# Two slots of a routed feed-forward layer started ahead of the last routing, V weights loaded in place, and the attention's values projected by channel

## Chip, core and metric

The kernel runs on one core of a Trainium2 chip. The metric is the device time of one launch, in microseconds (us). All tensors are float32; every large product is made of three matmuls of "fp32r" operands, a high part times high part, and the two products of a high with a low part.

## What is computed

Input x is 2 x 2048 x 256. The program is a feed-forward layer with three experts, a causal attention with one head of 128, and the same feed-forward layer again (same weights).

```python
x = x + 0.5 * ffn(layernorm(x)); x = x + attention(layernorm(x)); x = x + 0.5 * ffn(layernorm(x))
# ffn(x):
att = sigmoid(ln(x) @ Wr) * (ln(x) @ Wv) @ Wo;  state = ln(x) @ Ws;  x = x + att;  h = ln2(x)
bids = conf * shares * sigmoid(h @ w_diff) + h @ W_aff          # conf = sigmoid(h @ conf weights)
winner = argmax(bids)
hr[e] = square(relu(h @ K[e]));  out[e] = hr[e] @ V[e]          # experts 0, 1: 256 -> 1024 -> 256
out_trans = (h @ W1 * sigmoid(state @ W2)) @ W3                 # expert 2
return x + out[winner] * scale
```

## The kernel before, in words

Each feed-forward layer (FFN) has two stages. Stage A (ffn_a_*) goes over the 4096 rows in NG = 8 groups of 512, in a software pipeline written out by hand for each engine. For a group it makes the gates (U, Wo), the second normalization, its transpose hT, the bids, the W1 and W3 products of expert 2, and the rank of each row within expert 0 or 1 (prefix, rank). GpSimd scatters the finished rows (257 columns of h and index, 257 of residual and gate) with indirect DMAs to a DRAM array routed_rows, where the rows of expert 0 grow from one end and those of expert 1 from the other. Groups 0 to 5 are scattered whole (scatter, four DMAs of 128 rows), groups 6 and 7 in halves (scatter_half 0 and 1): half 0, what the expert products need, first; half 1 only when win_second and w3 on DVE have put the gate and expert 2's share into the rows (semaphore rdone).

Stage B (ffn_b_*) goes over NSLOT = 17 slots of 256 routed rows (the last of 128). DVE makes a table (flag, start) that says each slot's expert and first tile, from the number of rows of expert 1, known after the last group. SyncE loads the rows of a slot (slot_z: the h half; slot_row: the other half). For slot j, PE transposes (sT), ScalarE and DVE split the transpose into shT_hi and shT_lo (shi, slo), PE multiplies with K (Kj: four quarters of 12 matmuls of 256 columns in banks 1 to 4), ScalarE takes relu and hr_hi, DVE the square (sq), GpSimd hr_lo (hrlo), then PE multiplies with V (Vj: 48 matmuls), DVE adds the residual (orow) and GpSimd sends the rows with indirect DMAs (send). PE's order in a body is Kj(j), sT(j+1), Vj(j-1). sq of quarters 2 and 3 of slot j waits for hrlo of quarters 0 and 1 of the same slot (two buffers); on DVE slo(j+1) stands behind sq(j), and PE's Kj(j+1) waits for slo(j+1). On GpSimd a body is hrlo(j), a drain, send(j-1).

All orders are the order of the code. Before the change stage B begins when the table is done and the halves 0 of all groups have landed. In the first FFN the K, V and attention weights are loaded late in stage A (late_sync) into space that stage A has given back, and split into high and low parts by ScalarE (split_hi) and DVE (split_lo); the K bias is made by 64 matmuls of one column (k_bias). In the second FFN the weights are there.

The attention projects Q, K and V for 16 blocks of 256 rows (project_qk, project_v), eight ahead of the scores, the others one by one between them. project_v makes rows of values: 12 matmuls with a 128 x 128 tile of the normalized rows standing and 128 weight columns moving.

## Time and profile before

| what | us |
|---|---|
| three timed runs: median (lowest to highest) | 1061.05 (1060.47 to 1067.13) |
| the profiled execution, its own time | 1064.8 |
| its span (first to last instruction) | 1063.0 |
| first FFN (stage A to about 189, stage B to about 413) | 413 |
| attention | 413 to about 665 |
| second FFN (stage A to about 840) | 665 to 1063 |

The mean granted TensorE clock is 0.972 of full speed. In the rows below, times are us from the start of the span unless marked ns; PE is TensorE's matmul stream, PEld its weight loads, DVE is VectorE, ACT ScalarE, POOL GpSimd, SP SyncE. A row of the timeline gives start, duration, engine, line, operation, output<-inputs and count, and in brackets the idle time ahead of it and what ended it. Matmuls overlap in a pipeline, so the distance of two starts, not the duration, is what a matmul costs.

### The profile page before, as it was taken

What the parts mean: (1) busy time and instruction counts of PE and PEld (TensorE: products, weight loads), DVE (VectorE), ACT (ScalarE), POOL (GpSimd) and SP (SyncE); (2) the same over time, 40 slices, a digit from 0 to 9 for tenths busy, and PEclk for the clock granted to TensorE, in tenths of its full rate; (3) what the DMA queues carried; (4) which work ended last, traced back from release to release, by engine and by line L of the source; (5) the groups of instructions that cost most, each with busy time, mean ns of one, the idle gap of its engine ahead of it and who ended that gap; (6) DMA issues with size and microseconds to landing.
All of it is one profiled execution on the core that took longest, in us unless ns stands there. A gap on an engine that the chain in (4) does not pass through costs nothing.

```text
span 1063.0 us, 21617 instructions
## 1 busy us (share of the span) xinstructions
PE 988.0 (93%) x7024; PEld 912.5 (86%) x7025; DVE 688.6 (65%) x1762; ACT 560.1 (53%) x1185; POOL 488.4 (46%) x539
## 2 busy tenths in 40 slices
PE   8999998989999999889987998999999699999997
PEld 7788887989999998878886887778888599999997
DVE  5788877856555552656765667688887764555552
ACT  4767556354445551455543655676665255544452
POOL 3254544376556663821221001225634666666564
PEclk9999998799999999999999999999999799999999
DMA  8521243222122212201232134303112222212220
...
DMA packets 51237, 88.96 MB, mean 84 GB/s; under 512 B 5806, under 2 KB 43568, under 8 KB 49968
## 3 DMA queue, kind: packets, MB, share of 16 engines
...
## 4 chain that ended last, share of the span: by engine, by line
PE 64%; DVE 17%; ACT 6%; issue 5%; DMA 5%; POOL 4%; SPq 0%; DVEq 0%; POOLq 0%; ACTq 0%
PE banks4to L411 30%; PE bank L411 24%; PE banks4to L1715 3%; DVE out_rows L1057 2%; DMA attn_x<-x_after_ffn 2%; DVE pT_lo L1976 2%; DVE gT_lo L959 1%; PE bank L507 1%; DMA routed_rows<-out_rows,row_index 1%; PE bank L1258 1%; DVE zT_lo L948 1%; POOL attn_x L2069 1%; PE bank L1727 1%; PE bank L497 1%; DVE chunk_max L1966 1%
## 5 line engine op out<-in xcount | busy, mean ns | idle before, releaser
L1417 DVE TENSOR_TENSOR relu_squared<-relu 128x512 f32<-128x512 f32 (+1 forms) x136 | 151.0, 1124 | 108.3 <-ACT relu L1366 50.2
L1477 POOL TENSOR_TENSOR hr_lo<-relu_squared,hr_hi 128x512 fp32r<-128x512 f32 (+1 forms) x136 | 182.9, 1357 | 58.7 <-DVE relu_squared L1417 55.5
L1366 ACT ACTIVATE relu<-bank,slot_k_bias 128x256 f32<-128x256 f32 (+1 forms) x204 | 83.5, 460 | 176.6 <-PE bank L411 159.8
L411 PE MATMUL banks4to<-v_hi,hr_hi 128*128 128x256 f32 x528 | 151.8, 288 | 2.5 <-DVE slot_out L1426 2.5
L411 PE MATMUL banks4to<-v_hi,hr_lo 128*128 128x256 f32 x528 | 149.0, 282 | 0.0
L411 PE MATMUL banks4to<-v_lo,hr_hi 128*128 128x256 f32 x528 | 149.0, 282 | 0.0
L411 PE MATMUL bank<-shT_hi,k_hi 128*128 128x256 f32 (+1 forms) x408 | 117.5, 288 | 11.3 <-DVE shT_lo L1407 5.8
L411 PE MATMUL bank<-shT_hi,k_lo 128*128 128x256 f32 (+1 forms) x408 | 115.3, 283 | 0.0
L411 PE MATMUL bank<-shT_lo,k_hi 128*128 128x256 f32 (+1 forms) x408 | 115.2, 282 | 0.0
L411 PEld LDWEIGHTS banks4to<-v_hi,hr_hi 128*128 128x128 f32 x528 | 99.7, 189 | 2.9 <-issue 2.9
L884 POOL DMA_INDIRECT routed_rows<-out_rows,row_index x48 | 48.0, 999 | 116.9 <-DVE row_index L1040 105.9
L411 PEld LDWEIGHTS banks4to<-v_hi,hr_lo 128*128 128x128 f32 x528 | 99.8, 189 | 0.0
L411 PEld LDWEIGHTS banks4to<-v_lo,hr_hi 128*128 128x128 f32 x528 | 99.7, 189 | 0.0
L1374 ACT ACTIVATE hr_hi<-relu 128x512 fp32r<-128x512 f32 (+1 forms) x136 | 84.4, 620 | 15.9 <-ACT relu L1366 6.9
L411 PEld LDWEIGHTS bank<-shT_hi,k_hi 128*128 128x128 f32 x408 | 77.6, 190 | 14.9 <-issue 14.6
L411 PEld LDWEIGHTS bank<-shT_hi,k_lo 128*128 128x128 f32 x408 | 77.7, 190 | 0.0
L411 PEld LDWEIGHTS bank<-shT_lo,k_hi 128*128 128x128 f32 x408 | 77.6, 190 | 0.0
L1861 ACT CAST pT_hi<-bank 128x512 fp32r<-128x512 f32 (+1 forms) x72 | 39.1, 564 | 56.0 <-PE bank L1727 55.7
L1852 ACT ACTIVATE p<-banks4to,minus_row_max 128x512 f32<-128x512 f32 (+2 forms) x80 | 49.8, 628 | 28.8 <-DVE minus_row_max L1969 18.0
L1976 DVE TENSOR_TENSOR pT_lo<-bank,pT_hi 128x512 fp32r<-128x512 f32 (+1 forms) x72 | 46.2, 659 | 22.4 <-ACT pT_hi L1861 21.8
L1484 POOL DMA_INDIRECT x_after_ffn<-slot_out,token_index x33 | 34.6, 1049 | 52.9 <-DVE slot_out L1426 45.5
L1484 POOL DMA_INDIRECT out_x<-slot_out,token_index x33 | 32.8, 995 | 54.0 <-DVE slot_out L1426 45.0
...
## 6 DMA issues: line engine op xcount, KB each, us to landing
...
```

The lines of the kernel that those rows point to most:

```text
L411: mm = pe.matmul(outv, w(pw), m(pm), start=(n_first and k == 0), stop=(n_last and k == 2))
L884: pool.indirect_dma_start(routed, bass.IndirectOffsetOnAxis(b.posi[g % 2][:, t:t + 1].bitcast(U32), 0), b.rows[g % 2][:, t, :], None).then ...
L1057: last = dve.scalar_tensor_tensor(rows[:, t, RES], b.bank(6 + t // 2)[:, (t % 2) * C:(t % 2 + 1) * C], b.gt[p][:, t:t + 1], rows[:, t, RES ...
L1366: last = act.activation(b.r[q % 2][:, h % 2, 0:width(j)], b.bank(1 + q)[:, (h % 2) * SLOT:(h % 2) * SLOT + width(j)], ACT.Relu, bias=b.kbs ...
L1374: act.activation(b.hr[p][0][:, 2 * q:2 * q + 2, 0:width(j)], b.r[q % 2][:, :, 0:width(j)], ACT.Square).then_inc(f["hrhi"], 1)
L1417: dve.tensor_tensor(b.sq[q % 2][:, :, 0:width(j)], r, r, ALU.mult).then_inc(f["sq"], 1)
L1477: pool.tensor_tensor(b.hr[p][1][:, 2 * q:2 * q + 2, 0:n], b.sq[q % 2][:, :, 0:n], b.hr[p][0][:, 2 * q:2 * q + 2, 0:n].bitcast(F32), ALU.su ...
L1484: pool.indirect_dma_start(dst, bass.IndirectOffsetOnAxis(b.idx[p][:, t:t + 1].bitcast(U32), 0), b.o[p][:, t, :], None, bounds_check=N - 1, ...
L1715: mm = pe.matmul(out[:, at:at + n], b.kq[pw][:, q, 0, t * P:(t + 1) * P], part, start=(k == 0 and i == 0 and not last), stop=(k == 2), ski ...
L1852: act.activation(b.p[s % 2][t][:, c * KEYS:c * KEYS + w], bank(("S", s, t, c))[:, 0:w], ACT.Exp, bias=b.nbias[:, s % 2, t:t + 1], accum_ou ...
L1861: act.copy(b.pT[m % 2][0][:, 0:w], b.bank(m % 2)[:, 0:w]).then_inc(a["pthi"], 1)
L1976: dve.tensor_tensor(b.pT[m % 2][1][:, 0:w], b.bank(m % 2)[:, 0:w], b.pT[m % 2][0][:, 0:w].bitcast(F32), ALU.subtract).then_inc(a["ptlo"], 1)
```

## The change

1. A new DVE step first_slots, behind the rank of group 5, compares the rows of expert 1 in groups 0 to 5 with half of them. The expert with more rows gets slots 0 and 1, whose 512 rows lie at its end of routed_rows and are all there once group 5 has landed. SyncE loads slot_z of both at that point (semaphore early) and slot_row of both soon after. The table of the other slots (slot_table) is made later, for 15 slots.
2. PE transposes slots 0 and 1 (banks 1 and 2) behind the bids of group 7, and multiplies slots 0 and 1 with K (Kj(0), Kj(1)) ahead of W3 of group 7 (last_W3). DVE puts slo of both slots and g2 of group 7 ahead of the table, sq(0) ahead of win_second and w3 of group 6, and win_second and w3 of group 7 behind slo(2). GpSimd puts hrlo(0) ahead of half 1 of group 6, and half 1 of group 7 between hrlo(1) and send(0). The second FFN takes the same order.
3. The V weights come in one load of 2 MB to the place of v_lo (raw_v lies over it), in the first FFN's group loop, and are split in iterations 3 to 6 (one quarter each by ScalarE and DVE). late_sync is gone; the attention weights are loaded in the group loop too and split behind slot 1. The buffers of stage B move, so that none lies on what is still in use.
4. In the attention, project_v holds the weights still and moves 256 columns of z: 6 matmuls that give values by channel. ScalarE copies them to SBUF (v_turned), PE turns them with two transposes (turn_v), and the split follows as before. For the first eight blocks the products go to banks 0 to 3.

The order of instructions on three engines, at the places that matter (L numbers are lines of each version's own file).

GpSimd in the first FFN, before, from half 0 of group 7 to the first send (out_rows_65 is the buffer of odd groups, 64 of even ones; x_after_ffn<-slot_out is send):

```order
L874 DMA routed_rows<-out_rows_65,half_row_index 8448x257 x4
L874 DMA routed_rows<-out_rows_64,half_row_index 8448x257 x4
L1477 TENSOR_TENSOR hr_lo<-relu_squared_96,hr_hi 128x512
L1477 TENSOR_TENSOR hr_lo<-relu_squared_97,hr_hi 128x512
L1477 TENSOR_TENSOR hr_lo<-relu_squared_96,hr_hi 128x512
L1477 TENSOR_TENSOR hr_lo<-relu_squared_97,hr_hi 128x512
L874 DMA routed_rows<-out_rows_65,half_row_index 8448x257 x4
L1477 TENSOR_TENSOR hr_lo<-relu_squared_96,hr_hi 128x512
L1477 TENSOR_TENSOR hr_lo<-relu_squared_97,hr_hi 128x512
L1477 TENSOR_TENSOR hr_lo<-relu_squared_96,hr_hi 128x512
L1477 TENSOR_TENSOR hr_lo<-relu_squared_97,hr_hi 128x512
L1484 DMA x_after_ffn<-slot_out_98,token_index 4096x256 x2
```

and with the change (66 is the buffer of odd groups, 65 of even ones):

```order
L879 DMA routed_rows<-out_rows_66,half_row_index 8448x257 x4
L1546 TENSOR_TENSOR hr_lo<-relu_squared_95,hr_hi 128x512
L1546 TENSOR_TENSOR hr_lo<-relu_squared_96,hr_hi 128x512
L1546 TENSOR_TENSOR hr_lo<-relu_squared_95,hr_hi 128x512
L1546 TENSOR_TENSOR hr_lo<-relu_squared_96,hr_hi 128x512
L879 DMA routed_rows<-out_rows_65,half_row_index 8448x257 x4
L1546 TENSOR_TENSOR hr_lo<-relu_squared_95,hr_hi 128x512
L1546 TENSOR_TENSOR hr_lo<-relu_squared_96,hr_hi 128x512
L1546 TENSOR_TENSOR hr_lo<-relu_squared_95,hr_hi 128x512
L1546 TENSOR_TENSOR hr_lo<-relu_squared_96,hr_hi 128x512
L879 DMA routed_rows<-out_rows_66,half_row_index 8448x257 x4
L1553 DMA x_after_ffn<-slot_out_97,token_index 4096x256 x2
```

Half 1 of group 6 has moved behind the four hr_lo of slot 0, and half 1 of group 7 behind those of slot 1, directly ahead of send(0); the four hr_lo of slot 2 follow only then.

PE in the first FFN, before, where the slots begin (the six matmuls of g2T ahead are the end of W3 of group 7):

```order
L411 MATMUL banks4to<-w_hi,g2T_lo 128x256
L411 MATMUL banks4to<-w_lo,g2T_hi 128x256
L1258 MATMUL bank<-ident_sb,slot_z_90 128x128 x4
L1258 MATMUL banks4to<-ident_sb,slot_z_91 128x128 x4
L1284 TENSOR_LOAD slot_expert_int
L1284 ISA x2
L1288 COMPARE_AND_BRANCH
```

and with the change:

```order
L406 MATMUL bank<-hT_hi,w_lo 128x512
L406 MATMUL bank<-hT_lo,w_hi 128x512
L528 MATMUL bank<-ident_sb,bids_columns 128x128 x4
L1311 MATMUL bank<-ident_sb,slot_z_89 128x128 x4
L1311 MATMUL bank<-ident_sb,slot_z_90 128x128 x4
L406 MATMUL banks4to<-hT_hi,w_hi 128x512
L406 MATMUL banks4to<-hT_hi,w_lo 128x512
```

The transposes of slots 0 and 1 have moved from behind W3 of group 7 to behind the transpose of group 7's bids, ahead of the second half of its W1.

DVE in the second FFN, before, from the end of win_second of group 6 to g2T_lo of group 7:

```order
L1033 TENSOR_TENSOR trans_gate<-gate_work 128x4
L1034 TENSOR_TENSOR out_rows_64<-gate_work,trans_gate 128x4
L1057 SCALAR_TENSOR_TENSOR out_rows_64<-banks4to,trans_gate,out_rows_64 128x256 x4
L1048 SCALAR_TENSOR_TENSOR s_gate_63<-bank,bias_cols,s_gate_63 128x512
L1048 SCALAR_TENSOR_TENSOR s_gate_63<-banks4to,bias_cols,s_gate_63 128x512
L1170 TENSOR_TENSOR g2T_lo<-s_gate_63,g2T_hi 128x512 x2
```

and with the change, from the rank of group 7 on:

```order
L1047 SCALAR_TENSOR_TENSOR half_row_index<-banks4to,gate_work 128x4
L1048 SCALAR_TENSOR_TENSOR half_row_index<-banks4to,gate_work 128x4
L1479 TENSOR_TENSOR shT_lo<-bank,shT_hi 128x512 x2
L1082 SCALAR_TENSOR_TENSOR s_gate_64<-bank,bias_cols,s_gate_64 128x512
L1082 SCALAR_TENSOR_TENSOR s_gate_64<-banks4to,bias_cols,s_gate_64 128x512
L1197 TENSOR_TENSOR g2T_lo<-s_gate_64,g2T_hi 128x512 x2
L1065 COPY n_expert<-banks4to 128x1
L1066 TENSOR_TENSOR early_expert<-early_expert,n_expert 128x1
L1067 TENSOR_SCALAR slot_expert<-slot_row_sb,early_expert 128x14
```

and, behind the table, the squares of slot 0 with win_second and w3 of group 6:

```order
L1489 TENSOR_TENSOR relu_squared_95<-relu_93 128x512
L1489 TENSOR_TENSOR relu_squared_96<-relu_94 128x512
L1489 TENSOR_TENSOR relu_squared_95<-relu_93 128x512
L1489 TENSOR_TENSOR relu_squared_96<-relu_94 128x512
L1033 TENSOR_TENSOR gate_work<-gate_work 128x4
L1034 TENSOR_TENSOR gate_work<-gate_work 128x4
L1035 TENSOR_SCALAR gate_work<-gate_work 128x4
L1036 RECIPROCAL gate_work<-gate_work 128x4
L1037 SCALAR_TENSOR_TENSOR gate_work<-gate_work 128x4
L1038 TENSOR_TENSOR trans_gate<-gate_work 128x4
L1039 TENSOR_TENSOR out_rows_65<-gate_work,trans_gate 128x4
L1091 SCALAR_TENSOR_TENSOR out_rows_65<-banks4to,trans_gate,out_rows_65 128x256 x4
```

g2 and g2T_lo of group 7 are now ahead of the table and of w3 of group 6, and w3 of group 6 waits behind the four squares of slot 0.

The diff, cut to its core:

```diff
-        b.V = [sb(f"v_{p}", [P, 2, HC, C], F32R) for p in ("hi", "lo")]
+        v_hi = sb("v_hi", [P, 2, HC, C], F32R)
+        v_at = (nc.sbuf_base + 31) // 32 * 32
+        b.V = [v_hi, sb("v_lo", [P, 2, HC, C], F32R)]
+        b.raw_v = nc.alloc_sbuf_tensor_at("raw_v", [P, 2, HC, C], F32, offset=v_at)
...
 def ffn_a_sync(...):
         if s and g == X_BUFS:
+            sp.dma_start(b.raw_v[:].rearrange("p e a n -> p e (a n)"), v_w).then_inc(s.v, 16)
             for j in range(FILL, NSLOT):
                 fill(sp, f, pad, routed, j)
+        if s and g == X_BUFS + 2:
+            sp.dma_start(b.raw_a[:], w_qkv).then_inc(s.a, 16)
...
 def ffn_a_tensor(...):
     bidT(last)
+    slot_in(0, 0, 1)
+    slot_in(1, 1, 1)
     W1(last, 1, 2)
     W3(last - 1, range(0, 2))
     prefix(last)
     W3(last - 1, range(2, GT))
     if s:
+        pe.wait_ge(f["slo"], 2)
         k_bias(pe, b, s, 0)
         k_bias(pe, b, s, 1)
-    W3(last)
+    return lambda: W3(last)
...
 def ffn_a_scalar(...):
+        if s and k >= V_FROM:
+            act.wait_ge(s.v, 16)
+            split_hi(act, v_plan(b), k - V_FROM, k - V_FROM + 1, s.v_hi)
...
     conf(last)
+    shi(0, 0)
+    shi(1, 1)
...
 def ffn_a_vector(...):
+    def first_slots():
+        d, two = b.dirn[:, 0:1], slice(0, 2)
+        link(dve.tensor_scalar(d, b.bank(5)[:, 2 * GT:2 * GT + 1], float(GROUP * (NG - 2) // 2), None, ALU.is_ge))
...
+        if s and k >= V_FROM:
+            split_lo(dve, v_plan(b), k - V_FROM, k - V_FROM + 1, s.v_hi, s.v_lo)
     last = NG - 1
     rank(last - 2)
+    first_slots()
     lo(last - 1, f["hhi"], b.hT, f["hlo"])
...
     rank(last)
+    slot.lo(0, 0)
+    slot.lo(1, 1)
+    g2(last, 0)
+    g2(last, 1)
     if s:
         split_lo(dve, late, 0, K_ITEMS, s.k_hi, s.k_lo)
...
+    slot_table()
+    slot.sq(0, 0)
+    win_second(last - 1)
+    w3(last - 1)
...
 def ffn_b_sync(...):
+    sp.wait_ge(f["early"], 1)
     first = [rows_of(j, ST, slice(0, C)) for j in range(2)]
     for p in range(2):
-        sp.wait_ge(f["scat"][p], 16 * GT * NG // 2)
+        sp.wait_ge(f["scat"][p], 16 * GT * (NG - 2) // 2)
...
 def ffn_b_tensor(...):
         Kj(j, p, this)
+        if isinstance(j, int) and j == 1:
+            last_W3()
+            pe.wait_ge(f["flag"], 1)
+            if s:
+                pe.wait_ge(s.v_lo, V_ITEMS)
...
 def ffn_b_vector(...):
         if not last:
             slo(j + 1, 1 - p)
+        if isinstance(j, int) and j == 1:
+            last_rows()
         orow(j - 1, 1 - p, uses)
...
 def ffn_b_gpsimd(...):
     def body(j, p, last):
         hrlo(j, p)
+        if isinstance(j, int) and j == 1:
+            last_halves(NG - 1)
         pool.drain()
         send(j - 1, 1 - p)
 
     def first():
         hrlo(0, 0)
-        if last_halves:
-            last_halves()
+        last_halves(NG - 2)
...
 def attention_tensor(...):
     def project_v(k):
-        out = b.bank(k - QB + 4) if k in LATE_V else bank(("V", k))
+        out = b.bank(k % 4) if k < QB else bank(("V", k))
+        for c in range(CC):
+            mm = passes(pe, out[:, 0:SLOT], lambda p: b.Wvv[:, c, p * DK:(p + 1) * DK], lambda p: z_of(k)[p][:, c],
+                        c == 0, c == CC - 1)
+        mm.then_inc(a["V"], 1)
+
+    def turn_v(k):
+        pe.wait_ge(a["vt"], k + 1)
+        to = value_slot(k)
         for t in range(ST):
-            for c in range(CC):
-                mm = passes(pe, out[:, t * DK:(t + 1) * DK], lambda p: z_of(k)[p][:, c, t * P:(t + 1) * P],
-                            lambda p: b.Wvv[:, c, p * DK:(p + 1) * DK], c == 0, c == CC - 1)
-        mm.then_inc(a["V"], 1)
+            mm = pe.transpose(v_bank(b, k)[:, SLOT + t * DK:SLOT + (t + 1) * DK], b.vt[:, 2 * to + t], b.ident[:])
+        mm.then_inc(a["VN"], 1)
...
         weigh_some(s - 1, min(half + 2, n), n)
+        if ks:
+            turn_v(ks[0])
```

## Rows read from the trace of the kernel before

**Rows 1.** from the page, part 1 (busy us, share, instructions) and part 4 (chain)

```profile
PE 988.0 (93%) x7024; PEld 912.5 (86%) x7025; DVE 688.6 (65%) x1762; ACT 560.1 (53%) x1185; POOL 488.4 (46%) x539
...
PE 64%; DVE 17%; ACT 6%; issue 5%; DMA 5%; POOL 4%; SPq 0%; DVEq 0%; POOLq 0%; ACTq 0%
```

**Rows 2.** from the windows: length, busy (x) of PE, PEld, DVE, ACT, POOL, PEclk, DMA, GB/s

```profile
60.00:150.00 90.00, 88.31 (x538) 76.97 (x538) 75.91 (x249) 58.19 (x110) 42.84 (x61) 1.00 0.24 85
180.00:230.00 50.00, 44.89 (x296) 43.25 (x295) 36.81 (x91) 22.30 (x43) 28.59 (x24) 0.81 0.25 77
810.00:860.00 50.00, 38.30 (x229) 33.85 (x227) 36.33 (x143) 17.83 (x34) 25.34 (x27) 0.83 0.26 85
```

**Rows 3.** from PE's waits at 180 to 230 us (sum, times, longest)

```profile
PE bank L411 <- DVE shT_lo L1407: 4.7, 2, 3.5
PE banks4to L411 <- DVE g2T_lo L1170: 0.4, 1, 0.4
```

**Rows 4.** from PE's waits at 810 to 860 us

```profile
PE banks4to L411 <- DVE g2T_lo L1170: 6.8, 1, 6.8
PE bank L411 <- DVE shT_lo L1407: 1.1, 1, 1.1
```

**Rows 5.** from the chain that ended last (start, us): W3 of group 7, K products

```profile
199.91 5.17 PE banks4to L411 x24
...
228.44 6.04 PE bank L411 x36
...
242.40 4.50 PE bank L411 x36
...
254.47 4.50 PE bank L411 x36
...
884.77 4.51 PE bank L411 x36
```

**Rows 6.** from GpSimd's timeline, first slots of the first FFN

```profile
218.87 1.32 POOL L874 DMA_INDIRECT routed_rows<-out_rows,half_row_index  x1 [0.16 <-issue]
...
224.01 2.51 POOL L1477 TENSOR_TENSOR hr_lo<-relu_squared,hr_hi 128x512 fp32r<-128x512 f32 x2
...
232.60 1.29 POOL L1484 DMA_INDIRECT x_after_ffn<-slot_out,token_index  x1 [2.54 <-issue]
...
235.52 2.54 POOL L1477 TENSOR_TENSOR hr_lo<-relu_squared,hr_hi 128x512 fp32r<-128x512 f32 x2
```

**Rows 7.** from DVE's timeline, 211 to 217 us and 839 to 847 us

```profile
211.44 1.28 DVE L1417 TENSOR_TENSOR relu_squared<-relu 128x512 f32<-128x512 f32 x2
213.98 2.31 DVE L1417 TENSOR_TENSOR relu_squared<-relu 128x512 f32<-128x512 f32 x2 [1.26 <-POOL hr_lo L1477]
...
839.47 0.15 DVE L1149 COPY n_expert<-banks4to 128x1 f32<-128x1 f32 x1
...
841.30 0.15 DVE L1028 TENSOR_TENSOR gate_work<-gate_work 128x4 f32<-128x4 f32 x1
...
842.74 1.66 DVE L1057 SCALAR_TENSOR_TENSOR out_rows<-banks4to,trans_gate,out_rows 128x256 f32<-128x256 f32 x4
...
845.75 1.43 DVE L1170 TENSOR_TENSOR g2T_lo<-s_gate,g2T_hi 128x512 fp32r<-128x512 f32 x2
```

**Rows 8.** from DVE's timeline in the group loop, and from the groups by form

```profile
115.23 0.75 DVE L953 SCALAR_TENSOR_TENSOR r_gate<-bank,bias_cols,r_gate 128x512 f32<-128x512 f32 x1 [0.49 <-PE bank L411]
...
L402 DVE SCALAR_TENSOR_TENSOR v_lo<-raw_v,v_hi 128x1024 fp32r<-128x1024 f32 x4 | 4.6, 1219 | 0.0
```

**Rows 9.** from PE's timeline in the attention: a V projection and what follows

```profile
459.17 0.27 PE L411 MATMUL bank<-wv_hilo,attn_zT_hi 128*128 128x128 f32 x1
...
461.85 0.44 PE L1715 MATMUL banks4to<-kq_hi 128*128 128x512 f32 x1
```

**Rows 10.** from the page, part 5 (busy, mean ns, idle before): a ScalarE pass

```profile
L1366 ACT ACTIVATE relu<-bank,slot_k_bias 128x256 f32<-128x256 f32 (+1 forms) x204 | 83.5, 460 | 176.6 <-PE bank L411 159.8
```

**Rows 11.** from the chain that ended last: scattered rows on their way

```profile
151.16 6.08 DMA routed_rows<-out_rows,row_index
```

More of the change, by code:

```diff
@@ L1144, in ffn_a_vector @@
     residual(last)
+    if not s:
+        slot.kbs(0, 0)
+        slot.kbs(1, 1)
     bid_sum(last)
@@ L1208, in ffn_b_sync @@
     sp.wait_ge(f["late"], 16 * GT * 2)
-    for j in range(2):
-        row_in(j, j)
     with sp.Fori(0, (NSLOT - 5) // 2) as it:
@@ L1417, in sq, with ffn_b_vector @@
             dve.tensor_tensor(b.sq[q % 2][:, :, 0:width(j)], r, r, ALU.mult).then_inc(f["sq"], 1)
+    one.kbs, one.lo, one.sq = kbs, slo, sq
+    return one
+def ffn_b_vector(dve, b, f, s, slot, last_rows):
+    cr = b.carry["dve"]
+    n, base, kbs, slo, sq = slot.n, slot.base, slot.kbs, slot.lo, slot.sq
     def orow(j, p, uses):
@@ L1873, in attention_scalar @@
         qk_hi(k)
+        if 0 <= k - 1 and k - 1 not in LATE_V:
+            v_hi(k - 1)
         if k not in LATE_V:
-            v_hi(k)
+            v_turned(k)
         if k + 2 < QB:
@@ L2002, in attention_vector @@
         qk_lo(k)
-        if k not in LATE_V:
-            v_lo(k)
+        if 0 <= k - 1 and k - 1 not in LATE_V:
+            v_lo(k - 1)
         if k + 2 < QB:
@@ L2042, in attention_vector @@
             pair(s - 1, j)
+        for k in LATE_V if s == 0 else ks[:1]:
+            v_lo(k)
         for k in ks[1:]:
```

280 lines of the change are left out of this document (153 added, 127 removed).

## The prediction

> **What bounds the kernel now.** I read the page first: PE is busy 988 of 1063 us and holds 64% of the chain, DVE 17%, GpSimd 4% [rows 1]. So only time in which PE stands still, or matmuls that it need not make, can be won. The table by windows shows where PE stands still: in the group loop it is busy 88.3 of 90 us, at 180 to 230 us 44.9 of 50 and at 810 to 860 us 38.3 of 50 [rows 2]. These two are the passages from the last routing to the slots, and the granted clock falls there too, to 0.81 and 0.83. PE's waits name the causes. In the second FFN, W3 of group 7 waits 6.8 us for g2T_lo and the first K product 1.1 us for shT_lo [rows 4], because the routing, the table and w3 of group 6 stand ahead of g2T_lo on DVE. In the first FFN the waits are 0.4 us and 4.7 us in two, the longest 3.5 [rows 3]; that one is K(2), behind shT_lo of slot 2.
>
> Two consequences of a wait are seen in the chain. W3 of group 7 took 5.17 us for 24 matmuls behind k_bias, 0.215 each; a settled K product takes 4.50 us for 36, 0.125 each [rows 5]. That is the lower level of the clock (1.2 GHz) against the higher (2.4). And K(2), behind its wait of 3.5 us, took 6.04 us where K(3) took 4.50. I price a pass of 24 matmuls after k_bias at 5.17 - 3.0 = 2.2 us extra, and a wait of some us at 1.5 extra. Once it runs, a slot costs 12.07 us (242.40 to 254.47) [rows 5], 96 matmuls at 0.125: PE alone sets it.
>
> The baseline of each FFN is the start of K(3), which all later slots follow: 242.40 in the first, 884.77 in the second [rows 5].
>
> **The change, part by part.** A, V split in the group loop of the first FFN. It moves a pass of 1.22 us (128x1024) into each of four DVE bodies [rows 8]. The same body has a wait of 0.49 us for PE [rows 8], which covers that much; 1.22 - 0.49 = 0.73 is left, and as the first gate product waits for it, PE loses it. The fourth split falls in the last routing, where PE's bids are late anyway, so 3 x 0.73 = +2.2 us. Bounds: 0 if DVE's body has other slack (it is busy 75.9 of 90 us [rows 2]); if each pass also waits for GpSimd's g2T_lo (the shape of hr_lo, 2.54 for two, 1.27 each [rows 6]), 3 x (0.73 + 1.27) = 6.0. The load of 2 MB goes where the DMA engines are busy about a quarter of the time [rows 2]; I count it as hidden behind the groups.
>
> B, the passage in the first FFN. PE's order is now W3(6), k_bias, K(0), K(1), W3(7). k_bias, its cost and the low clock behind it remain; the low clock now hits K(0) instead of W3(7), the same 2.2 us. Before, PE came to W3(7) 0.4 us ahead of 199.9 [rows 3, 5], so at 199.5. Eight transposes of slots now stand ahead, at the 0.112 of a 128-column matmul (2.68 us for 24 [rows 9]), 0.9 us: K(0) 200.4 to 208.6, K(1) to 214.6. DVE has made its first three squares in the meantime, and the fourth ends about 210.6. win_second and w3 of group 6 then take 1.4 and 1.7 us (841.30 to 842.74, and 1.66 [rows 7]): 213.7. GpSimd's half 1 of group 6 takes 5.14 us (218.87 to 224.01 [rows 6]): 218.9. Its first hr_lo of slot 1 releases squares, these shT_lo of slot 2, and K(2) came 4.4 us behind it (224.01, and 228.44 [rows 5, 6]): K(2) at 223.3. PE, with W3(7) and V(0) behind K(1), is ready at 214.6 + 3.0 + 0.5 + 6.0 = 224.1, so here it hardly waits.
> Then comes the new link. hr_lo of slot 1 takes 6.05 us (224.01 to 230.06, which is 232.60 less 2.54 [rows 6]) and ends at 225.0. Half 1 of group 7 waits for last_rows, which stands on DVE behind slo(2) (about 223.3) and takes 3.1: 226.4. Four issues, 5.1: 231.5. Then a drain. Behind hr_lo the first send stood 2.54 us [rows 6]; behind bare DMA issues nothing shows it: 0 if it finds nothing to wait for, 6.1 if it waits for the rows to land (6.08 [rows 11]). I take 1.0, between 0 and the 2.54 of the nearest row. Send(0), 2.9 (232.60 to 235.52): 235.4. K(3) is 4.4 behind: 239.8. PE is ready at 224.1 + 12.1 = 236.2 and waits 3.6, which costs 1.5 by the clock. Against 242.40: -2.6 + 1.5 = -1.1. Queued behind half 1 of group 7 are send(0) and all hr_lo of slot 2, and behind these DVE's squares and PE; that is why this queue decides.
>
> C, the passage in the second FFN. PE reached its wait at 847.2 - 6.8 = 840.4 (g2T_lo: 845.75 + 1.43 [rows 4, 7]); with the transposes 841.3. K(0) to 847.3, K(1) to 853.3. DVE comes to the old place of the table at 839.5. Two shT_lo, two s_gate (844.4 to 845.75) and g2T_lo take 1.4 each: 843.7. The table, 1.8 (839.47 to 841.30): 845.5. Four squares with their wait for hr_lo, 4.85 (211.44 to 216.29): 850.4. win_second and w3, 3.1: 853.5 [rows 7]. W3(7) needs the banks that this w3 reads, so PE starts it 0.2 late, and V(0) ends at 863.0. Half 1 of group 6: 853.6 to 858.7. K(2) at 863.1. hr_lo(1) ends at 864.8; last_rows, behind slo(2), at 866.1; half 1 of group 7 at 871.2, drain 872.2, send 875.1, K(3) 879.5. PE is ready at 863.1 + 12.1 = 875.2 and waits 4.3, with 1.5 of clock. Against 884.77: -5.3 + 1.5 = -3.8.
> The first-slot comparison is some nine small DVE steps of 0.15 us at most one after the other, as the table's (0.15 [rows 7]); they stand behind the rank of group 5, ahead of group 6's and 7's work, where DVE waits for PE. I count 0; uncovered they would cost about 1.4 in each FFN.
>
> D, attention. 24 matmuls of 128 columns, two projections of a block of 256 rows, took 2.68 us [rows 9]: 1.34 for one. Now it is 6 of 256 columns, 6 x 0.125 = 0.75, and two transposes, 0.22. Gain 0.37 each. Over 16 blocks: 5.9. The copy by ScalarE stands between product and transposes; one of 128x256 takes 0.46 [rows 10], 0.9 with its hand-overs (an estimate: twice the pass). Where blocks come between few scores, PE waits for it. The first eight gain 3.0; of the late eight I let five lose 0.5 each: -3.0 + 2.5 = -0.5. Bounds: -5.9, and 8 x (0.9 - 0.37) = +4.2 if all the late ones lose and the first gain nothing.
>
> **Sum.** +2.2 - 1.1 - 3.8 - 0.5 = -3.2. The profiled execution took 1064.8 (1063.0 of span and 1.8 around it); the sum makes it 1061.6. The median of the runs is 1061.05, 3.7 below it; the same change gives 1057.9.
>
> **A rule that speaks against it.** Two squares beside GpSimd's hr_lo took 2.31 us, two alone 1.28 [rows 7]; such DVE passes lengthen when GpSimd works. The Trainium skill, page "SBUF — State Buffer", section "SBUF: two separate sides", says that a DVE operation with two SBUF inputs and a GpSimd operation that reads SBUF exclude each other for the whole instruction. This trace agrees as far as those 2.31 go. By the rule v_lo, with two inputs, would stop at each g2T_lo of GpSimd, and the upper bound of A would hold. No row shows v_lo beside g2T_lo.
>
> **Rivals.**
> 1. GpSimd's queue does not bind: hrlo and send overtake nothing late, K(3) follows PE. Then all waits go. First FFN: 4.7 + 0.4 + 1.5 = 6.6. Second: 6.8 + 1.1 + 2.2 = 10.1. Sum 2.2 - 6.6 - 10.1 - 0.5 = -15.0: 1046.0. For it: GpSimd is 4% of the chain and 46% busy. Against: K(2) waited 3.5 us already with half as much ahead of it [rows 3, 6]. Chance 0.26.
> 2. The slower side: the drain waits until half 1 of group 7 has landed, 6.1 instead of 1.0. Both K(3) are 5.1 later: B +4.0, C +1.3; sum 2.2 + 4.0 + 1.3 - 0.5 = +7.0: 1068.1. It turns the sign as soon as the drain costs over 2.6 (3.2 / 2 on top of 1.0). For it: 2.54 us of unexplained idle before the first send. Against: scatters to DRAM have their own semaphores, and the steps of the loop show no 6 us. Chance 0.12.
> 3. V splits stopped by GpSimd, A = 6.0: sum +0.6, 1061.7. Chance 0.12.
> 4. The attention gains everything, D = -5.9: sum -8.6, 1052.5. Chance 0.14.
>
> **How the numbers follow.** The forecast, 1057.9, has 0.36 and its own range 1052 to 1063, the rest the rivals. A measurement of this kernel can tell about 1%, 10.6 us, from no change: under 1050.4 is faster, over 1071.7 slower. Faster is rival 1 (0.26) and a twelfth of the others together, 0.32; slower only the drain with other misses, 0.04; the rest, 0.64, is within 1%. The range of 8 in 10 runs from 1045 (rival 1 with a little more) to 1066 (rival 3 and part of rival 2).
>
> **What would show it.** In the profile after: in the second FFN K(0) begins near 841 and W3 of group 7 no longer waits; K(3) begins near 239.8 + A and near 879.5 plus what the time before it moved. PE has one wait of 3 to 5 us for shT_lo just ahead of K(3), and on GpSimd half 1 of group 7 and send(0) stand directly ahead of hr_lo of slot 2. In the group loop, DVE's v_lo takes 1.22 us and a group becomes 0.7 longer in three periods. In the attention a V projection and its transposes take 0.97 us of PE. No wait ahead of K(3) makes rival 1 right, one of 8 us or more rival 2. The forecast is wrong if slots cost another time than 12.07, or if slots 0 and 1 start later than W3(6) ends, because their rows came late.

## The result, and the profile after

| what | before | with the change |
|---|---|---|
| median of 7 timed runs, us | 1063.43 | 1072.33 |
| lowest to highest, us | 1060.47 to 1067.13 | 1069.09 to 1075.48 |
| ratio to before (95% interval) | | 1.0070 (1.0052 to 1.0088) |
| the profiled execution; its span, us | 1064.8, 1063.0 | 1069.1, 1067.2 |

The change makes the kernel slower by 0.7%, some 7.4 us by the ratio (the medians of the seven differ by 8.9). The forecast was 1057.9 us, 3.2 faster, with a range of 1045 to 1066; the 1072.33 measured lie outside it. The profiled execution is the fastest of the seven with the change, and shows 4.3 of these 7.4 us; the table at the end of this section comes back to this.

The page, part 1 (busy us, share, instructions by engine) and part 4 (shares of the chain), against [rows 1]:

```profile
PE 978.6 (92%) x6962; PEld 904.1 (85%) x6963; DVE 692.2 (65%) x1780; ACT 565.1 (53%) x1201; POOL 488.2 (46%) x539
...
PE 61%; DVE 20%; issue 6%; ACT 6%; POOL 5%; DMA 2%; POOLq 0%; SPq 0%; DVEq 0%; ACTq 0%
```

PE is busy 9.4 us less (4.6 of them in the attention, at 420 to 660 us, which has fewer matmuls; k_bias, at a higher clock, takes 2.2 less), and the span is 4.2 longer, so PE stands still some 13.6 us more. GpSimd's share of the chain went from 4 to 5%, DVE's from 17 to 20%.

The windows of [rows 2], and two more, which lie right behind the two passages:

```profile
60.00:150.00 90.00, 87.38 (x537) 76.77 (x536) 78.84 (x252) 60.88 (x113) 45.72 (x60) 1.00 0.25 86
180.00:230.00 50.00, 47.72 (x348) 46.08 (x348) 36.06 (x94) 22.35 (x47) 25.52 (x22) 0.89 0.20 63
230.00:260.00 30.00, 21.63 (x159) 21.34 (x158) 12.19 (x23) 8.65 (x19) 16.87 (x15) 0.83 0.22 67
810.00:860.00 50.00, 42.44 (x288) 38.41 (x287) 40.65 (x150) 27.13 (x55) 26.49 (x26) 0.97 0.25 80
860.00:900.00 40.00, 32.25 (x254) 32.08 (x253) 19.11 (x34) 12.85 (x27) 25.07 (x22) 0.87 0.20 61
```

and the two that are added, before:

```profile
230.00:260.00 30.00, 29.63 (x242) 29.28 (x241) 16.64 (x32) 15.29 (x33) 19.33 (x16) 0.97 0.27 78
860.00:900.00 40.00, 39.77 (x335) 39.50 (x334) 22.54 (x35) 21.97 (x47) 26.07 (x21) 1.00 0.20 56
```

At 180 to 230 us and 810 to 860 us PE is busier than before (47.7 and 42.4 of 50 us, before 44.9 and 38.3). The loss has moved into the stretch behind: at 230 to 260 us PE is busy 21.6 us for 29.6 before, at 860 to 900 us 32.3 for 39.8. PE's waits (sum, times, longest) in the first FFN, at 180 to 260 us, against [rows 3]:

```profile
PE bank L406 <- DVE shT_lo L1479: 9.2, 2, 8.4
PE banks4to L406 <- DVE out_rows L1091: 1.3, 1, 1.3
```

and in the second, at 840 to 890 us, against [rows 4]:

```profile
PE bank L406 <- DVE shT_lo L1479: 7.7, 1, 7.7
PE banks4to L406 <- DVE out_rows L1091: 3.1, 1, 3.1
```

The 6.8 us for g2T_lo are gone. In their place stand one wait of 8.4 and one of 7.7 us for shT_lo, and a smaller one of W3 of group 7 for w3 of group 6 (1.3 and 3.1 us). The chain, start and duration of K products, against [rows 5]:

```profile
243.28 7.12 PE bank L406 x36
...
258.03 4.47 PE bank L406 x36
...
886.30 6.54 PE bank L406 x36
...
900.58 4.54 PE bank L406 x36
```

K(3) starts at 243.3 and 886.3 (before 242.4 and 884.8), and its 36 matmuls in the chain take 7.12 and 6.54 us where settled ones take 4.5: the granted clock at 243 to 250 us is 0.56, before it was 1.00 there. GpSimd's timeline in the first FFN, against [rows 6], shows what K(3) waited for:

```profile
221.57 2.83 POOL L1546 TENSOR_TENSOR hr_lo<-relu_squared,hr_hi 128x512 fp32r<-128x512 f32 x2 [0.70 <-DVE relu_squared L1489]
227.79 0.98 POOL L879 DMA_INDIRECT routed_rows<-out_rows,half_row_index  x1 [3.38 <-DVE out_rows L1091]
...
231.87 0.96 POOL L879 DMA_INDIRECT routed_rows<-out_rows,half_row_index  x1 [0.30 <-issue]
236.19 1.00 POOL L1553 DMA_INDIRECT x_after_ffn<-slot_out,token_index  x1 [3.36 <-issue]
...
238.48 2.51 POOL L1546 TENSOR_TENSOR hr_lo<-relu_squared,hr_hi 128x512 fp32r<-128x512 f32 x2
```

From above: the last hr_lo of slot 1; 3.38 us idle until w3 of group 7 is done; the first and the last of the four issues of half 1; 3.36 us idle, put down to issue, which is the drain (the first two experiments show it); send(0); and only then the first hr_lo of slot 2, 14 us after the last of slot 1 ended (224.40). DVE's squares 2 and 3 of slot 2, shT_lo of slot 3 and K(3) hang on it.

Where the profiled pair drifts apart (start of the same instruction, with the change less before):

| PE instruction | before | after | difference |
|---|---|---|---|
| bids of group 5, first FFN | 152.86 | 153.09 | +0.2 |
| k_bias | 188.26 | 189.41 | +1.2 |
| transposes of slot 4 | 248.17 | 251.68 | +3.5 |
| end of the first FFN | 416.07 | 420.39 | +4.3 |
| last transpose of the attention | 661.15 | 664.07 | +2.9 |
| first transpose of the second FFN's loop | 666.64 | 669.00 | +2.4 |
| last transpose of bids, second FFN | 834.86 | 834.55 | -0.3 |
| K(3) | 884.77 | 886.30 | +1.5 |
| transposes of slot 4 | 890.54 | 894.13 | +3.6 |
| last matmul | 1058.53 | 1062.70 | +4.2 |

Each FFN loses 4.3 to 4.5 us between its last routing and its end, together 8.8; most of it stands at the transposes of slot 4 already, and 0.8 and 0.6 us are lost in the slots behind, for which no run here has a reason. Between the two the profile gains 4.6: 2.0 from the end of the first FFN to the first transpose of the second, 0.6 in the groups behind, and 2.0 in the stretch from group 7's first transpose to the last bids of the second FFN. That stretch took 41.3 us before and 39.2 here; in the profiles of the experiments it took 39.2 once and 40.4 to 41.3 in eleven, ten of them with the same code there as the changed kernel. So nearly all of these 2.0 go with the granted clock (0.83 at 820 to 840 us before, 1.00 here) and not with the change. The timed runs, 7.4, lie between the profiled 4.3 and the 8.8 of the two FFNs alone.

### The profile page after: what moved, and what is told of

It is laid out like the page before. It is cut to its first block, busy times and chain, and to the rows that moved or that the text cites. A ratio compares the mean times of both kernels' runs of the same rounds, so it can differ in the third digit from the quotient of the medians.

```text
span 1067.2 us, 21537 instructions
## 1 busy us (share of the span) xinstructions
PE 978.6 (92%) x6962; PEld 904.1 (85%) x6963; DVE 692.2 (65%) x1780; ACT 565.1 (53%) x1201; POOL 488.2 (46%) x539
## 4 chain that ended last, share of the span: by engine, by line
PE 61%; DVE 20%; issue 6%; ACT 6%; POOL 5%; DMA 2%; POOLq 0%; SPq 0%; DVEq 0%; ACTq 0%
PE banks4to L406 27%; PE bank L406 23%; PE banks4to L1794 3%; DVE out_rows L1091 2%; DVE pT_lo L2074 2%; PE bank L506 1%; DVE gT_lo L964 1%; DVE chunk_max L2064 1%; POOL routed_rows L879 1%; PE bank L1806 1%; DVE zT_lo L953 1%; ACT p L1946 1%; PE bank L1311 1%; DMA attn_x<-x_after_ffn 1%; DVE r_gate L958 1%
## 5 line engine op out<-in xcount | busy, mean ns | idle before, releaser
L1546 POOL TENSOR_TENSOR hr_lo<-relu_squared,hr_hi 128x512 fp32r<-128x512 f32 (+1 forms) x136 | 180.1, 1336 | 58.2 <-DVE relu_squared L1489 54.5
L406 PE MATMUL bank<-shT_hi,k_hi 128*128 128x256 f32 (+1 forms) x408 | 120.0, 294 | 22.4 <-DVE shT_lo L1479 17.0
L406 PE MATMUL bank<-shT_hi,k_lo 128*128 128x256 f32 (+1 forms) x408 | 117.8, 289 | 0.0
L406 PE MATMUL bank<-shT_lo,k_hi 128*128 128x256 f32 (+1 forms) x408 | 117.7, 288 | 0.0
L406 PEld LDWEIGHTS bank<-shT_hi,k_hi 128*128 128x128 f32 x408 | 81.0, 198 | 25.8 <-issue 25.4
L406 PEld LDWEIGHTS bank<-shT_hi,k_lo 128*128 128x128 f32 x408 | 81.0, 198 | 0.0
L406 PEld LDWEIGHTS bank<-shT_lo,k_hi 128*128 128x128 f32 x408 | 80.9, 198 | 0.0
```

What stands on the lines that cost most here:

```text
L406: mm = pe.matmul(outv, w(pw), m(pm), start=(n_first and k == 0), stop=(n_last and k == 2))
L1546: pool.tensor_tensor(b.hr[p][1][:, 2 * q:2 * q + 2, 0:n], b.sq[q % 2][:, :, 0:n], b.hr[p][0][:, 2 * q:2 * q + 2, 0:n].bitcast(F32), ALU.su ...
```

## The experiments

The theory is that GpSimd's queue sets the start of a K product: whatever stands there between the last hr_lo of one slot and the first of the next delays it (theory Q). Each run is timed against the kernel before on its chip, and the number is the ratio to it, with the 95% interval. The changed kernel itself is at 1.0070 (1.0052 to 1.0088); what one run gains over another is the difference of two such ratios, good to 2 or 3 us. Two kernels, with two drains and with a second V split, ran once, for their traces.

**The drain ahead of half 1 of group 7.**

```diff
         hrlo(j, p)
+        pool.drain()
         if isinstance(j, int) and j == 1:
             last_halves(NG - 1)
-        pool.drain()
         send(j - 1, 1 - p)
```

> The changed kernel, with GpSimd's drain of the body of slot 1 ahead of half 1 of group 7 instead of behind it. Theory Q (GpSimd's queue of hr_lo(1), half 1, drain, send(0), hr_lo(2) sets K(3) in both FFNs): the drain now falls into the 3.4 us in which GpSimd waits for w3 of group 7, the 3.3 us idle ahead of send(0) becomes about 0.3, K(3) starts 3.0 us earlier in both FFNs (240.3 and, with the first FFN's gain behind it, 880.3), and the time falls by about 6 against the changed kernel. Rival P (PE or its low clock sets K(3), the queue has slack): the idle goes, K(3) moves by less than 1 us, the time by less than 2.

Measured 1.0009 (0.9993 to 1.0024), 6.5 us less than the changed kernel. GpSimd, the last issue and send(0):

```profile
228.78 0.99 POOL L879 DMA_INDIRECT routed_rows<-out_rows,half_row_index  x1 [3.39 <-DVE out_rows L1091]
...
232.86 0.96 POOL L879 DMA_INDIRECT routed_rows<-out_rows,half_row_index  x1 [0.30 <-issue]
234.13 1.00 POOL L1553 DMA_INDIRECT x_after_ffn<-slot_out,token_index  x1 [0.30 <-issue]
```

The idle time ahead of send(0) is 0.30, and the wait for w3 of group 7 is unchanged at 3.39: the drain is hidden in it. PE waited 5.3 us instead of 8.4 for K(3) in the first FFN and 4.9 instead of 7.7 in the second, and K(3) came 2.1 and 2.8 us earlier (241.2 and 883.5). Q holds, and the place of one drain, twice in the program, was worth most of the loss. It was not worth more: with the drain hidden the kernel is level with the one before, not faster.

**What the drain waits for.** The changed kernel with a second drain directly behind the first:

```diff
             last_halves(NG - 1)
+            pool.drain()
         pool.drain()
```

> The changed kernel with a second drain directly behind the first, in the body of slot 1 on GpSimd. If the drain waits for the rows of half 1 to be written (or for any work in flight), the second finds nothing, and the idle ahead of send(0) stays at 3.3 us. If a drain has a fixed cost of about 2.5 to 3 us, the idle becomes 5 to 6 us and K(3) 2 to 3 us later.

GpSimd's timeline, the last issue and send(0):

```profile
232.61 0.96 POOL L879 DMA_INDIRECT routed_rows<-out_rows,half_row_index  x1 [0.30 <-issue]
236.84 1.00 POOL L1553 DMA_INDIRECT x_after_ffn<-slot_out,token_index  x1 [3.27 <-issue]
```

The idle stays at 3.27. So the drain has no fixed cost of that size: it waits until something that is under way is done, and a second one finds nothing to wait for. Whether this is the landing of the rows is not shown, but the times fit it. SyncE issues its first load of residual rows once the late halves have landed, in the changed kernel at

```profile
235.63 0.37 SPq L1233 DMA_DIRECT2D slot_row<-routed_rows  x1
```

2.8 us behind the end of the last issue (232.83). GpSimd's queue took up the next instruction of its own at 235.41, 0.2 us before; in the second FFN, and twice in the kernel with two drains, the two were 0.2 us apart as well. The 6.1 us of [rows 11] are then too long for these rows. On the other side, the kernel before has 2.54 us idle behind its drain when these rows had landed long before (SyncE issued that load at 226.3, hr_lo ended at 230.1), and the slot_out that send(0) sends was ready at 230.9; so such rows aren't all that an idle time there can stand for.

**Half 1 of group 7 inside hr_lo(2).**

```diff
     def hrlo(j, p):
         for q in range(HC // 2):
+            if isinstance(j, int) and j == 2 and q == 2:
+                last_halves(NG - 1)
...
         hrlo(j, p)
-        if isinstance(j, int) and j == 1:
-            last_halves(NG - 1)
         pool.drain()
```

> The changed kernel, with half 1 of group 7 between the second and third hr_lo of slot 2, so that nothing but send(0) stands between hr_lo(1) and the first hr_lo of slot 2. Theory Q: send(0) starts near 228.7 in the first FFN, K(3) near PE's own readiness, 235 to 236 (before 243.3), its wait of 8.4 us falls under 1 us, and the first K product behind it is at full clock; the same in the second FFN, so -9 or so in each, 18 against the changed kernel, if nothing else binds. Rival W (a new wait): half 1 lands later, SyncE loads the h half of slot 4 only behind it, near 248, and PE waits for that load at the transposes of slot 4, due at 241: the wait moves from K(3) to there, about 6 us of it remain in each FFN, and the time falls by only 5 to 8.

Measured 1.0033 (1.0017 to 1.0050), 4 us less than the changed kernel and less than either theory gave (18, or 5 to 8). K(3) came at 235.9, as Q says, but a new wait of PE took its place in both FFNs:

```profile
PE bank L1311 <- DMA slot_z<-routed_rows: 5.0, 1, 5.0
PE bank L406 <- DVE shT_lo L1479: 1.8, 2, 1.0
```

PE waits 5.0 us (4.8 in the second FFN) at the transposes of slot 4 for their load, which SyncE issues only when the late halves have landed. Q held for K(3), W for what came next.

**The same, with the load of slot 4 freed from the late halves.**

```diff
-    for j in range(2, 4):
+    for j in range(2, 5):
         z_in(j, j % 2)
     sp.wait_ge(f["late"], 16 * GT * 2)
-    with sp.Fori(0, (NSLOT - 5) // 2) as it:
+    with sp.Fori(0, (NSLOT - 7) // 2) as it:
         for par in range(2):
             row_in(it * 2 + 2 + par, par)
-            z_in(it * 2 + 4 + par, par)
+            z_in(it * 2 + 5 + par, 1 - par)
+    row_in(PAIRS - 4, 0)
+    z_in(PAIRS - 1, 1)
+    row_in(PAIRS - 3, 1)
     row_in(PAIRS - 2, 0)
```

> As the kernel with half 1 of group 7 inside hr_lo(2), and SyncE loads the h half of slot 4 before it waits for the late halves (the loop of loads is shifted by one slot). Theory Q: no wait of PE over 1 us from K(0) to slot 5, K(3) near 235.5 and 876, the time 16 to 20 under the changed kernel and about 10 under the kernel before. Rival W: if this is no faster than the kernel without the earlier load, the load was not what bound there; if it is 5 to 8 faster, it was.

Measured 0.9954 (0.9933 to 0.9974), and in a second session:

> The kernel with half 1 of group 7 inside hr_lo(2) and the h half of slot 4 loaded ahead of the late halves, once more, as the reference of the next two on the same chip: a ratio of 0.995 to before, as measured, if that was no accident of the chip.

0.9962 (0.9946 to 0.9978). This is 11 to 12 us under the changed kernel and 4 to 5 under the one before. The order of GpSimd and one load, with the rest of the change as it was, turn its sign. Of the 16 to 20 us that Q gave, these are two thirds: K(3) came at 236.7 and 875.0, but K(4) still waited 2.5 and 1.9 us. Half 1 now stands for 5.1 us (872.90 to 877.99) ahead of the last two hr_lo of slot 2 and of send(1), and through them slot 3's come late; no run tells this share from that of what came before on GpSimd. PE's timeline in the second FFN has it, the start of K(3) and of K(4):

```profile
875.02 0.35 PE L406 MATMUL bank<-shT_hi,k_hi 128*128 128x256 f32 x1 [0.65 <-DVE shT_lo L1482]
...
889.09 0.51 PE L406 MATMUL bank<-shT_hi,k_hi 128*128 128x256 f32 x1 [1.89 <-DVE shT_lo L1482]
```

**Both halves 1 inside.** Two kernels start from the last one. Half 1 of group 6 too goes between the second and third hr_lo, of slot 1; in the first of the two, win_second and w3 of group 6 also go ahead of the squares of slot 0 (the last six lines of the edit, which the second of the two doesn't have).

```diff
-            if isinstance(j, int) and j == 2 and q == 2:
-                last_halves(NG - 1)
+            if isinstance(j, int) and j in (1, 2) and q == 2:
+                last_halves(NG - 3 + j)
...
         hrlo(0, 0)
-        last_halves(NG - 2)
...
     slot_table()
-    slot.sq(0, 0)
     win_second(last - 1)
     w3(last - 1)
+    slot.sq(0, 0)
```

> That kernel, and also half 1 of group 6 between the second and third hr_lo of slot 1, and win_second and w3 of group 6 ahead of the squares of slot 0. Theory Q (what stands on GpSimd between two slots' hr_lo sets the next K product): W3 of group 7 no longer waits for w3 of group 6 (1.0 and 3.1 us now), K(2) loses its 0.9 in the first FFN, and K(3) and K(4) come 1 to 3 us earlier; 3 to 6 us less than the kernel without this. Rival R (GpSimd's work is only moved: eight issues of 1.3 us and the sends still pass through it before slot 4): the waits move from W3 and K(2) to K(3) and K(4), and the time changes by under 1.5 us.

> The kernel with both halves 1 inside hr_lo(1) and hr_lo(2), and win_second and w3 of group 6 left behind the squares of slot 0. With them ahead the ratio was 0.988, without either move 0.996. Theory Q alone (GpSimd's order makes the gain): 0.990 or less, and W3 of group 7 still waits 3.1 us in the second FFN. Rival (the order on DVE makes it): 0.994 to 0.996.

Both moves: 0.9879 (0.9858 to 0.9899), a median of 1051.38 us beside 1063.72 on its chip. Only GpSimd's: 0.9882 (0.9865 to 0.9900). GpSimd's order makes the whole gain. GpSimd's timeline of the first shows what stands where now, hr_lo of slot 1, half 1 of group 6, and hr_lo again:

```profile
849.89 2.87 POOL L1551 TENSOR_TENSOR hr_lo<-relu_squared,hr_hi 128x512 fp32r<-128x512 f32 x2 [0.78 <-DVE relu_squared L1492]
852.91 1.25 POOL L879 DMA_INDIRECT routed_rows<-out_rows,half_row_index  x1 [0.16 <-issue]
...
857.00 0.96 POOL L879 DMA_INDIRECT routed_rows<-out_rows,half_row_index  x1 [0.30 <-issue]
857.99 2.55 POOL L1551 TENSOR_TENSOR hr_lo<-relu_squared,hr_hi 128x512 fp32r<-128x512 f32 x2
862.74 1.01 POOL L1558 DMA_INDIRECT out_x<-slot_out,token_index  x1 [2.20 <-issue]
...
865.04 1.32 POOL L1551 TENSOR_TENSOR hr_lo<-relu_squared,hr_hi 128x512 fp32r<-128x512 f32 x1
```

PE's waits in the second FFN with both moves:

```profile
PE bank L406 <- DVE shT_lo L1482: 4.2, 2, 2.3
PE banks4to L406 <- DVE out_rows L1091: 0.8, 1, 0.8
```

and with GpSimd's move alone:

```profile
PE banks4to L406 <- DVE out_rows L1091: 3.1, 1, 3.1
```

With DVE's move the 3.1 us of W3 of group 7 are gone, but K(3) and K(4) wait 4.2 together for shT_lo (2.3 and 1.9), which they don't with GpSimd's move alone (0.2 and 0.5, put down to issue). For DVE's move rival R was right: the wait only moves. For GpSimd's Q was, and the 8 to 9 us over the kernel with one half inside are more than the 3 to 6 expected. In the first FFN K(4) still waits 2.1 us for shT_lo in both.

**win_second ahead of the squares, in the changed kernel.**

```diff
     slot_table()
-    slot.sq(0, 0)
     win_second(last - 1)
+    slot.sq(0, 0)
     w3(last - 1)
```

> The changed kernel, with win_second of group 6 (seven DVE steps on 128x4) ahead of the squares of slot 0 instead of behind them. In the changed kernel the first two of these steps took 1.25 and 1.21 us, beside GpSimd's hr_lo, where they take 0.16 elsewhere. Theory L (a DVE step with two inputs and a GpSimd step exclude each other): ahead of the squares no hr_lo runs, both steps take 0.16, w3 of group 6 ends 2.2 us earlier, W3 of group 7 waits 0.9 instead of 3.1 in the second FFN, half 1 of group 6 and through it K(3) come about 2 us earlier in both FFNs, the time falls by about 4 against the changed kernel. Rival (the 1.25 us are the latency of a chain of dependent steps, wherever it stands): nothing moves but the squares, 1.4 later, and the time is the same or 1 to 2 longer.

Measured 1.0037 (1.0017 to 1.0057), 3.5 us less than the changed kernel. The first two steps of win_second in the changed kernel, behind the squares:

```profile
850.66 1.25 DVE L1033 TENSOR_TENSOR gate_work<-gate_work 128x4 f32<-128x4 f32 x1
851.95 1.21 DVE L1034 TENSOR_TENSOR gate_work<-gate_work 128x4 f32<-128x4 f32 x1
```

GpSimd's timeline beside them:

```profile
850.28 2.85 POOL L1546 TENSOR_TENSOR hr_lo<-relu_squared,hr_hi 128x512 fp32r<-128x512 f32 x2 [0.69 <-DVE relu_squared L1489]
```

and ahead of them:

```profile
846.34 0.16 DVE L1033 TENSOR_TENSOR gate_work<-gate_work 128x4 f32<-128x4 f32 x1
846.53 0.16 DVE L1034 TENSOR_TENSOR gate_work<-gate_work 128x4 f32<-128x4 f32 x1
```

1.25 and 1.21 us against 0.16. As they depend on each other in the same way in both places, it isn't their latency; what differs is hr_lo beside them. W3 of group 7 waited 0.95 instead of 3.1 us in the second FFN, and K(3) came 1.5 us earlier in the first FFN and, counted from the last bids, 2.6 in the second. The Trainium skill, page "SBUF — State Buffer", section "SBUF: two separate sides", has such operations exclude each other for the whole instruction; these rows agree: each of the two steps took about as long as one hr_lo beside it (2.85 us for two), where 0.16 us are its own.

**A second V split in the group loop.** A DVE pass of the same form as v_lo, 1.22 us, is added ahead of it in the four bodies of the kernel with half 1 of group 7 inside and the load of slot 4 freed.

```diff
         if s and k >= V_FROM:
+            dve.wait_ge(s.v_hi, k - V_FROM + 1)
+            raw_n, _, hi_n, _ = v_plan(b)[k - V_FROM]
+            dve.scalar_tensor_tensor(b.K[1][:, 0, 0].rearrange("p (a n) -> p a n", a=HC // 2), raw_n, 1.0, hi_n.bitcast(F32),
+                                     ALU.mult, ALU.subtract)
             split_lo(dve, v_plan(b), k - V_FROM, k - V_FROM + 1, s.v_hi, s.v_lo)
```

> The kernel with half 1 of group 7 inside hr_lo(2), with a second DVE pass of the form of v_lo (128x1024, 1.22 us) in each of the four bodies that split V, its result in space not yet used. Forecast A's premise (DVE is on the path in the group loop): the period of a group, 20.5 us, grows by about 1.2 in three iterations, the start of k_bias by 3.7. Theory S (DVE has slack there, the waits for PE of 0.5, 0.2 and about 1 us in a body): the start of k_bias moves by under 1 us. A lock between this pass and GpSimd's g2T_lo would show as a later g2T_lo on GpSimd, not as a longer pass on DVE.

k_bias starts at 191.1 instead of 189.0 and 189.5 in the two profiles of that kernel, 1.7 to 2.2 us later for 4.9 us of added work. DVE is near the path but not on it: the first pass cost about nothing, the second about 0.5 a body. This lies between the two expectations. v_lo kept its 1.22 us on DVE; it was GpSimd that gave way. Its timeline in the changed kernel:

```profile
112.75 1.16 POOL L864 TENSOR_TENSOR rsqrt_work<-rsqrt_work 128x4 f32<-128x4 f32 x1
113.87 2.54 POOL L868 TENSOR_TENSOR g2T_lo<-s_gate,g2T_hi 128x512 fp32r<-128x512 f32 x2
```

and at the same place before:

```profile
112.75 0.20 POOL L859 TENSOR_TENSOR rsqrt_work<-rsqrt_work 128x4 f32<-128x4 f32 x1
112.90 2.54 POOL L863 TENSOR_TENSOR g2T_lo<-s_gate,g2T_hi 128x512 fp32r<-128x512 f32 x2
```

The product of 128x4 took 1.16 us instead of 0.20 beside v_lo (112.64 to 113.86 on DVE), and g2T_lo started 1.0 later. With the second pass on DVE (114.73 to 115.95) g2T_lo itself takes 3.53 us instead of 2.54:

```profile
114.83 3.53 POOL L868 TENSOR_TENSOR g2T_lo<-s_gate,g2T_hi 128x512 fp32r<-128x512 f32 x2
```

**The old attention.** In two kernels, the changed one and the one with half 1 of group 7 inside and the load of slot 4 freed, the attention's functions on PE, ScalarE and DVE are those of before:

```diff
...
-        for c in range(CC):
-            mm = passes(pe, out[:, 0:SLOT], lambda p: b.Wvv[:, c, p * DK:(p + 1) * DK], lambda p: z_of(k)[p][:, c],
-                        c == 0, c == CC - 1)
+        for t in range(ST):
+            for c in range(CC):
+                mm = passes(pe, out[:, t * DK:(t + 1) * DK], lambda p: z_of(k)[p][:, c, t * P:(t + 1) * P],
+                            lambda p: b.Wvv[:, c, p * DK:(p + 1) * DK], c == 0, c == CC - 1)
...
```

> The changed kernel with the attention of the kernel before (values projected by rows, 24 matmuls of 128 columns per two blocks, no turn). Forecast of the term D: the new attention gains 0.5, so this would be 0.5 slower than the changed kernel. Reading of the two profiles: from the end of the first FFN to the first transpose of the second the gap of 4.3 us between the kernels falls to 2.4, so this would be about 2 slower. Rival (full gain of 0.37 at each of 16 blocks): 5.9 slower.

> The kernel with half 1 of group 7 inside hr_lo(2), with the attention of the kernel before. Forecast D: 0.5 us slower than the same kernel with the new attention (the profiles of the first pair gave 0.5 between the first and the last transpose of the attention). Rival: full gain, 5.9 slower. Rival: none or a loss, 0 to 4 faster.

Measured 1.0085 (1.0052 to 1.0117) beside 1.0070, and 0.9970 (0.9953 to 0.9987) beside 0.9962 on the same chip: slower by about 1.6 and 0.9 us with the old attention, both within the intervals (the medians of the first pair even differ the other way, 1.0069 and 1.0084). The full gain of 5.9 is excluded by the second pair; a gain of 0.5 and none at all cannot be told apart.

**The kernel before, with half 1 of group 7 inside hr_lo(1).** Does Q hold where the change isn't?

```diff
         for q in range(HC // 2):
+            if last_halves and isinstance(j, int) and j == 1 and q == 2:
+                last_halves()
...
         hrlo(0, 0)
-        if last_halves:
-            last_halves()
```

> The kernel before, with half 1 of group 7 in the first FFN moved from ahead of hr_lo(1) to between its second and third (nothing else). Theory Q holds of that kernel too: K(2) loses its wait of 3.5 us and the low clock behind it, 1.5, so -4 to -5 us or a ratio of 0.9955. Rival W: the other halves of slots 0 and 1 are loaded 5 us later, orow(0) with them, and V(1) waits as much as K(2) gained: a ratio of 0.999 to 1.002.

Measured 0.9982 (0.9970 to 0.9995). PE's waits in the first FFN, against [rows 3]:

```profile
PE banks4to L411 <- DVE slot_out L1426: 3.8, 1, 3.8
PE bank L411 <- DVE shT_lo L1407: 1.2, 1, 1.2
```

K(2) came at 224.8, 3.6 us earlier and without a wait, and V(1) waited 3.8 us for slot_out of slot 0: K(3) stood at 242.7, as before (242.4). DVE's timeline has what slot_out waited for:

```profile
233.69 0.17 DVE L1424 COPY token_index<-slot_row 128x2 int32<-128x2 int32 x1 [9.49 <-DMA slot_row<-routed_rows]
```

Rival W: in the kernel before, the late halves bind through the residual rows that the first sends need. The 2 us gained lie between the 4 to 5 of Q and W's nothing, nearer to W. The changed kernel loads the residual rows of slots 0 and 1 before these halves, so this wait can't arise there; what that alone is worth was not run.

## Why the prediction was wrong, point by point

- **What bounds the kernel: right for the two passages.** The waits that the change aims at are gone. But the passages held only 17 of the 75 us in which PE stood still; 27 lay at 420 to 660 us, in the attention.
- **The link half 1, drain, send(0), hr_lo(2), K(3) as what is late next: right in kind, too short in size.** This is the step that failed, in B and C: the time from w3 of group 7 through half 1, the drain and send(0) to K(3), and above all the drain, put at 1.0. In the first FFN I had K(3) at 239.8, and it came at 243.3. hr_lo(1) ended 0.6 earlier than worked out. Half 1 of group 7 began at 227.8, not 226.4: slo(2) was done 0.7 earlier, but the first two steps of win_second took 0.6 and 1.2 us beside hr_lo instead of 0.16 each, and 0.8 passed between the end of w3 on DVE (227.0) and GpSimd's start, which I had put at nothing. The drain took 3.36, not 1.0. The first hr_lo to K(3) took 4.8, not 4.4, the sends 0.6 less. Together 1.4 + 2.4 + 0.4 less 0.6 and 0.1 are the 3.5 us. In the second FFN (879.5, and 886.3) both halves paid these: w3 of group 6 ended at 855.8 and not 853.5 (so W3 of group 7 waited 3.1 us and not 0.2), the hand-over took 0.8 more, half 1 of group 7 began 4.8 late, and the drain was 2.3 longer.
- **"I take 1.0" for the drain, between 0 and the 2.54 of the nearest row.** No row gave that value. The row itself was the nearest, and with it B and C would have been 1.5 later each. Rival 2 had the mechanism (the drain waits for something in flight), with 6.1; 3.3 is what it took. Its point of turning, 2.6, was passed, and its sign (a wait of 8 us or more ahead of K(3)) was there with 8.4 and nearly with 7.7; it had the chance of 0.12. By the sum the sign of the forecast hung on this term, but the drain alone doesn't explain it: with the drain hidden the kernel is at 1.0009, where the sum without a drain gives 5.2 us of gain. What is left are the hand-overs, the slow steps of win_second and the clock; of these only the steps were tried by themselves (3.5 us).
- **The price of the low clock behind a wait: too low.** I took 1.5 for any wait of some us. Behind 8.4 and 7.7 us the next K product took 7.12 and 6.54, that is 2.6 and 2.0 more, and the slot took 14.7 instead of 12.1 us (243.28 to 258.03).
- **A, the V split: wrong, on the safe side.** +2.2 forecast, 0.2 measured at group 5 and nothing by the last bids of the first FFN (182.84 before, 182.72 after; 182.6 to 183.3 in the profiles of the other kernels with one split). The body had more slack than the one row of 0.49 us shows. The load of 2 MB and the first-slot steps, counted as 0, are in these numbers and were hidden too. Rival 3 had the lock with its direction reversed: GpSimd waits for v_lo, and GpSimd has time there.
- **k_bias** starts 1.2 later (0.9 forecast, for the eight transposes) and is 2.2 us shorter (9.05 for 11.24, the granted clock of 190 to 200 us is 0.73 for 0.54), which I had not in the sum. It took 8.9 to 10.2 us in the profiles of ten other kernels with the change and 11.3 in the one with a second V split, 11.2 and 11.5 in the two without, so it seems to go with the change; why is not shown. K(0) then took 5.69 for its 36 matmuls in the chain, 1.2 over a settled one, where I had 2.2. K(1) ended at 211.5 for 214.6; K(3), set by GpSimd's queue, got nothing of that.
- **D, attention: -0.5 forecast,** -0.9 and -1.6 by two pairs of runs that don't exclude 0: nothing speaks against it. Its working leaves out three of the eight late blocks; with their gain of 0.37 each it would have been -1.6. Rival 4 is out.
- **Rival 1 is out** as a description of this kernel, yet its time, 1046, tells what was there to be had: with both halves inside hr_lo the kernel takes 1051.4 to 1052.3.
- **The sum.** A and B were to cost 1.1 together and cost 4.3; C was to gain 3.8 and lost 4.5; with D at -0.5 that makes +8.3 for the -3.2 forecast, beside 7.4 measured by the ratio. About half of the 11.5 us between the two is the drain (2.4 and 2.3) and the clock behind the longer wait (1.1 and 0.5). Another 2.4 us of the distance from 1057.9 to 1072.3 are not of the change: the forecast stood on a median of three runs, 1061.05, and that of seven is 1063.43.
